# Local attention in blocks of 32 queries and 96 keys, with the probabilities turned on VectorE

## The chip, the core and the metric

The kernel runs on one core of a Trainium2 chip, as one launch. The metric is device time in microseconds, from the start of the program to its end. The core has a matrix engine (TensorE, PE in the profile), VectorE (DVE), ScalarE (ACT), GpSimd (POOL), and a queue on SyncE (SP) that issues transfers. Each engine runs its own instruction stream in order; the streams meet at semaphores.

## The reference, cut to what matters

The input is x, 8 sequences of 1024 rows of 128 numbers. The result comes from three steps, all in fp32:

```
x = x + 1/2 * block(LN(x)); x = x + causal_attention(LN(x)); x = x + 1/2 * block(LN(x))
block: 2 layers of
    h = shift_token(x)                    # the second half of the columns comes from the row before
    q, k, v = split(h @ wqkv)             # 8 heads of 64
    q, k = rotary_xpos(l2norm(q) * qs, l2norm(k) * ks)
    sim = q k^T * 8, masked where key > query or key < query - 64
    x = x + softmax(sim) v @ wo           # wo: 512 x 128
    h = LN(shift_token(x)) * g + b
    a, gate = split(h @ w1 + b1)          # 2 x 341 columns
    x = x + (a * gelu(gate)) @ w2 + b2
```

What the change touches is `softmax(sim) v @ wo`. A query sees itself and the 64 keys before it, 65 keys in all.

## The kernel before

The four local layers (two before the causal attention, two after it) are cut into turns of 256 rows: 32 turns a layer, 128 in all. A loop `local(phase)` on each engine does a *round*, which is two turns, t and t+1; the work of a round is spread over five neighbouring turns (index t-4 to t), so that every engine always has work of several turns at hand. The first and last rounds of each phase, and the causal attention between them, are written out with the same functions. There are 64 pairs of turns in all.

The order of the instructions on each engine is written by hand, as the order of the calls in these loops. The accumulators lie in 8 PSUM banks. The table `ROTA` says which results use a bank in a round, in which order; `vacant` makes PE wait until the engine that reads the former user is done.

The chain of the local attention in one turn, with its lines in the profile:

- `project` (L619 to L621) makes q, k and v of 128 rows, three fp32r matmuls each (high and low parts of both sides). VectorE, POOL and ACT square, rotate and normalise q and k, and `turn` (L628) transposes them on PE into QT2 and KT.
- `scores(t, i)` (L644, L652), for 128 queries and two banks (even heads, odd heads): four bf16 matmuls put the mask into the banks, and 16 fp32 matmuls add q k^T in tiles of 64x64 of the array, each for 64 queries and 128 keys. An fp32 matmul stands in the trace as two records.
- `row_max` (DVE, L2248, one per bank, four a turn), `exp_rows` (ACT, L4440, four of 128x128 per bank), `row_inverse` (DVE, L2254, four a turn) and `scale_p` (POOL, L5792, 128x512) make the probabilities P.
- `turn_p` (PE, L662) transposes P in 16 pieces of 128x128 a turn into four PSUM banks P0 to P3, and `copy_p` (ACT, L4447) copies each bank to PT.
- `copy_v` (ACT, L4430) puts v into VP, and `move_v` (SP, L537 to L543) fills the other 64 partitions of it with three or four transfers of 128 KB a turn, so that 128 keys stand on 128 partitions for each 64 queries.
- `values(t, i)` (L678), twice a turn: 16 fp32 matmuls of 128 keys x 64 columns (32 records) into one bank O0 or O1.
- `split_o` (ACT, L4454) rounds the result to OTH, `rest_of_o` (DVE, L2260) makes the remainder OTL, and `wo` (L690 to L692) does 12 fp32r matmuls a turn.

What follows keeps its work: `turn_rows` and `turn_back` (the transposes around L702 and L718), LN, `to_gate` and `to_up` (L723 to L725), `gelu`, `gate`, `down` (L742), and the transposes of L756.

## Time and profile before

| | |
|---|---|
| median of 3 runs | 2623.92 us (2622.96 to 2627.61) |
| the profiled execution | span 2623.2 us from first to last instruction; no total of its own is given |
| TensorE clock, mean over the span | 0.993 of full speed |
| PE busy | 2558.0 us, 98% |
| VectorE busy | 2376.0 us, 91% |
| ScalarE busy | 2346.8 us, 89% |
| POOL busy | 2056.4 us, 78% |
| DMA, mean busy share of the 16 engines | queue q1 13.1% |
| transfers that lay out V | 480, 128.0 KB each |

The table is from the first part of the page. Busy time is the union of an engine's instructions. A row of the timeline gives the start, the time until the last of the group has ended, and the engine, line and shapes; since instructions of one engine overlap (the next starts before the last has left the pipeline), the cost of one is read from start to start. In a list of waits each row gives the total, the count and the longest.

### The profile page before, as it was taken

The page shows a single profiled execution, that of the slowest core. Times are in us where ns is not written, and L with a number is a line of the kernel's source. Part 1 is how long each engine was busy: PE and PEld are TensorE (multiplying, and loading weights), DVE is VectorE, ACT ScalarE, POOL GpSimd, SP SyncE. Part 2 cuts the span into 40 slices and gives each one's busy share as a digit, 9 for nine tenths or more (in the row PEclk, how much of TensorE's full clock was granted, in tenths as well). Part 3 has the DMA queues.
Part 4 walks back from the last instruction along what each step waited for, and adds up shares of the span by engine and source line. Part 5 has one row for each costly group of instructions (what it writes and reads, how often), then busy time and mean ns, then how long its engine had stood idle before and what let it go on. Part 6 is the DMA issues. An engine that isn't in the chain of part 4 may idle for free.

```text
span 2623.2 us, 80275 instructions
## 1 busy us (share of the span) xinstructions
PE 2558.0 (98%) x29132; PEld 2063.6 (79%) x29132; DVE 2376.0 (91%) x6206; ACT 2346.8 (89%) x7379; POOL 2056.4 (78%) x2185
## 2 busy tenths in 40 slices
PE   5999999999999999998999999999999999999998
PEld 4778777877788888886997777778777788888876
DVE  7999999999999999996888999999998999999995
ACT  5999999999999999995555999999999999999996
POOL 7999999988887877872104999999988888787873
PEclk8999999999999999999999999999999999999999
DMA  4121111111111111110000111111111111111110
GB/s 105 44 51 31 28 38 31 28 28 39 24 32 28 28 42 26 32 28 8 9 1 11 32 28 32 26 38 32 29 24 39 28 32 40 30 40 36 36 40 26
DMA packets 63810, 83.95 MB, mean 32 GB/s; under 512 B 11538, under 2 KB 30652, under 8 KB 63420
## 3 DMA queue, kind: packets, MB, share of 16 engines
q1 hardware_dynamic: 63420, 78.82, 13.1%
q8 instruction: 236, 3.87, 0.6%
q14 instruction: 154, 1.26, 0.2%
HBM read 11.67 MB, written 4.19 MB: 6 GB/s over the span
## 4 chain that ended last, share of the span: by engine, by line
PE 83%; POOL 6%; DVE 5%; ACT 4%; issue 2%; SPq 0%; DMA 0%; ACTq 0%; POOLq 0%; DVEq 0%
PE PS L678 8%; PE PS L662 8%; PE PS L628 7%; PE PS L652 7%; PE PS L619 6%; PE PS L742 6%; PE PS L621 6%; PE PS L620 6%; PE PS L723 4%; PE PS L725 3%; PE PS L724 3%; PE PS L644 3%; PE PS L690 2%; PE PS L853 2%; PE PS L692 2%
## 5 line engine op out<-in xcount | busy, mean ns | idle before, releaser
L4440 ACT ACTIVATE P<-PS,MX 128x128 f32<-128x128 f32 x2048 | 754.3, 430 | 2.1 <-DVE MX L2248 1.2
L5756 POOL TENSOR_TENSOR T<-T,SQ 128x512 f32<-128x512 f32 x512 | 652.1, 1284 | 115.3 <-DVE SQ L2209 111.7
L5792 POOL TENSOR_TENSOR P<-P,RI 128x512 f32<-128x512 f32 x512 | 527.8, 1042 | 73.8 <-DVE RI L2254 71.7
L4440 ACT ACTIVATION_READ_ACCUMULATOR P<-PS,MX 128x1 f32 x2048 | 535.6, 268 | 0.0
L5769 POOL TENSOR_TENSOR T<-T,RN 128x512 f32<-128x512 f32 x512 | 525.9, 1048 | 6.2 <-DVE RN L2242 3.8
L2190 DVE TENSOR_REDUCE SS<-SQ 128x8 f32<-128x512 f32 x512 | 343.8, 681 | 44.6 <-ACT SQ L4395 37.9
L4395 ACT ACTIVATE SQ<-PS 128x512 f32<-128x512 f32 x512 | 338.1, 662 | 45.9 <-PE PS L621 35.0
L619 PE MATMUL PS<-WH,YH 128*128 128x512 f32 x768 | 346.1, 451 | 6.9 <-POOL YL L5745 3.3
L2248 DVE TENSOR_REDUCE MX<-PS 128x4 f32<-128x512 f32 x512 | 345.8, 678 | 6.5 <-PE PS L652 6.3
L2209 DVE TENSOR_TENSOR SQ<-PS,TAB 128x512 f32<-128x512 f32 x512 | 349.1, 682 | 2.3
L2201 DVE TENSOR_TENSOR T<-PS,TAB 128x512 f32<-128x512 f32 x512 | 344.2, 682 | 7.1 <-PE PS L628 3.3
L4447 ACT COPY PT<-PS 128x512 f32<-128x512 f32 x512 | 301.9, 626 | 32.1 <-PE PS L662 32.0
L628 PEld LDWEIGHTS PS<-CST,T 128*128 128x128 f32 x2048 | 238.6, 141 | 88.8 <-issue 54.8
L628 PE MATMUL PS<-CST,T 128*128 128x128 f32 x2048 | 292.4, 275 | 14.0 <-POOL T L5769 13.4
L621 PE MATMUL PS<-WH,YL 128*128 128x512 f32 x768 | 305.3, 397 | 0.0
L620 PE MATMUL PS<-WL,YH 128*128 128x512 f32 x768 | 303.4, 395 | 0.0
L662 PE MATMUL PS<-CST,P 128*128 128x128 f32 x2048 | 296.4, 278 | 3.1 <-POOL P L5792 1.0
L678 PEld LDWEIGHTS PS<-PT,VP 128*64 128x64 f32 x8192 | 249.5, 138 | 28.3 <-issue 28.1
L662 PEld LDWEIGHTS PS<-CST,P 128*128 128x128 f32 x2048 | 229.2, 141 | 52.4 <-issue 22.9
L652 PE MATMUL PS<-KT,QT 64*64 64x128 f32 x8192 | 268.6, 269 | 0.0
L678 PE MATMUL PS<-PT,VP 128*64 128x64 f32 x8192 | 267.3, 224 | 0.0
L652 PEld LDWEIGHTS PS<-KT,QT 64*64 64x64 f32 x8192 | 243.4, 133 | 16.9
(155 smaller groups left out, 5938.4 us busy)
## 6 DMA issues: line engine op xcount, KB each, us to landing
VP<-VP SPq DMA_DIRECT2D x480, 128.0 KB, 2.3
out_dram<-X SPq DMA_DIRECT2D x16, 256.0 KB, 2.6
X<-in_L_attn_x_dram SPq DMA_DIRECT2D x7, 512.0 KB, 4.5
SG<-in_L_ffn_w_dram SPq DMA_DIRECT2D x5, 341.0 KB, 3.0
...
```

The costliest lines, as they stand in the source:

```text
L619: pe.matmul(PS[:, b, :], YH[:, k, :], WH[:, cols], start=True, stop=False)
L620: pe.matmul(PS[:, b, :], YH[:, k, :], WL[:, cols], start=False, stop=False)
L621: pe.matmul(PS[:, b, :], YL[:, k, :], WH[:, cols], start=False, stop=True).then_inc(projected[x], 1)
L628: ins = pe.transpose(PS[:, b, 128 * p:128 * p + 128], T1[:, k, 128 * p:128 * p + 128], ident)
L652: ins = pe.matmul(PS[64 * w:64 * w + 64, bank_of(f"S{2 * i + x}", t), 128 * p:128 * p + 128], QT2[at, s, p, m:m + WIN], KT[at, p, k:k + 12 ...
L662: ins = pe.transpose(PS[:, b, 128 * p:128 * p + 128], P[:, g, p, :], ident)
L678: ins = pe.matmul(PS[64 * x:64 * x + 64, b, 128 * p + m:128 * p + m + WIN], VP[:, s, 2 * i + w, d:d + 64], PT[:, 2 * i + x, p, m:m + WIN], ...
L2209: dve.tensor_tensor(SQ[:, (2 * n + 1 - x) % 3, :].rearrange("p (h t d) -> p h t d", h=HEADS, t=2), PS[:, b, :].rearrange("p (h t d) -> p h ...
L4440: ins = act.activation(P[:, g, p, :], PS[:, b, 128 * p:128 * p + 128], ACT.Exp, bias=MX[:, g, p:p + 1], accum_out=SM[:, g, p:p + 1])
L5756: pool.tensor_tensor(T1[:, k, :], T1[:, k, :], SQ[:, (2 * n + 1 - x) % 3, :], ALU.add).then_inc(added[x], 1)
L5769: pool.tensor_tensor(heads, heads, RN[:, t % 2, i, 8 * x:8 * x + 8].unsqueeze(2).broadcast_to([128, HEADS, DH]), ALU.mult).then_inc(scaled ...
L5792: pool.tensor_tensor(P[:, g], P[:, g], RI[:, g, :].unsqueeze(2).broadcast_to([128, NPAIR, 128]), ALU.mult).then_inc(p_scaled, 1)
```

## The change

Local attention works in blocks of 32 queries and 96 keys where it had 64 queries and 128 keys. In parts:

- `scores`: one mask matmul for each of 8 array tiles (64 rows x 32 columns), 384 columns wide (L583, L585), then 32 fp32 matmuls (64 records) of 96 columns per 128 queries (L591). The tiles of four pairs of heads stand side by side in the array, so that the queries of a head pair lie on 32 partitions of the bank.
- `row_max` and `row_inverse` work on both banks in one instruction, two a turn each (L1502, L1509). `exp_rows` runs over 96 columns, `scale_p` over 384.
- `turn_p` is now on VectorE (L1516): four STREAM_TRANSPOSE a turn, 128x384, which turn each 32x32 piece in place and write PT directly. `copy_p` and the banks P0 to P3 are gone; banks O2 and O3 are new.
- `values(t)` is one call for a turn (L610): 76 or 80 fp32 matmuls (152 or 160 records) of 32 keys, with 32, 64 or 96 columns, in 8 tiles of 32 rows x 64 columns; for each tile the columns of one turn sum to 768 in two passes.
- `copy_v` writes to a staging buffer VT; `move_v(t)` lays it out in a ring VR by 16 transfers of 32 KB a turn (L480). All wait for both copies of the turn; the last eight also wait for `values(t-1)`.
- `wo` is 4 plain fp32 matmuls of 256 columns (8 records, L623). `split_o` copies two banks in one instruction to a double buffer OT. `rest_of_o`, the high and low parts of Wo and `zero_v` are gone.
- The orders of all engines, `ROTA` and its tables are new. The loops run rounds 3 to 31 and 35 to 63 in place of 9 to 31 and 41 to 62.

PE's round is now: K projection of (t-3,1), two turns of (t-4,1), V projection of (t-4,1), `wo(t-5)`, `scores(t-4,1)`, V of (t-3,0), K of (t-2,0), `turn_rows`, V of (t-3,1), two turns, Q of (t-2,0), `scores(t-3,0)`, K of (t-2,1), `turn_back`, `values(t-4)`; then a turn, Q, gate, a turn, gate, V, an LN transpose, `scores(t-3,1)`, gate, up, up, K, up, `wo(t-4)`, `down`, Q, `values(t-3)`, two turns, Q, LN and y transposes, `scores(t-2,0)`.

```diff
+QB, KB = 32, 96
+NB = 128 // QB
+BPC = CH // QB
+BACK = WIN // QB
+RING = 2 * BPC
+PTS, PTW = 2, BPC * KB + 64
...
-ROUNDS = {0: (9, 32), 1: (41, 63)}
+ROUNDS = {0: (3, 32), 1: (35, 64)}
...
-    [("P0", 4), ("P3", 4), ("YT", 4), ("S3", 3), ("V0", 1), ("S3", 2)],
+    [("V0", 3), ("K0", 2), ("O2", 4), ("LT", 1), ("NR", 2), ("O3", 3), ("S1", 2)],
...
-        def move_v(t, i):
-            s = t % 2
-            on.wait_ge(v_copied, TPC * t + i + 1)
-            sp.dma_start(VP[64:128, s, 2 * i, :], VP[0:64, s, 2 * i + 1, :]).then_inc(v_moved[s][i], 16)
-            if i > 0:
-                on.wait_ge(v_copied, TPC * t + 1)
-                sp.dma_start(VP[0:64, s, 2, :], VP[64:128, s, 1, :]).then_inc(v_moved[s][i], 16)
-            elif not first(t):
-                on.wait_ge(v_copied, TPC * t)
-                sp.dma_start(VP[0:64, s, 0, :], VP[64:128, 1 - s, WPC - 1, :]).then_inc(v_moved[s][i], 16)
+        def move_v(t):
+            on.wait_ge(v_copied, TPC * (t + 1))
+            on.wait_ge(valued, t - 1)
...
+            for k in range(NB):
+                if k == NB - BACK:
+                    on.wait_ge(valued, t)
+                for c in range(NPAIR):
+                    sp.dma_start(VR[QB * c:QB * c + QB, slot(t, k):slot(t, k) + NB + 1:NB, :],
+                                 VT[QB * k:QB * k + QB, t % 2, :, 128 * c:128 * c + 128]).then_inc(v_moved[t % 4], 16)
...
-            for w in range(2):
-                v = 1 if first(t) and i == 0 and w == 0 else 0
-                for x in range(2):
-                    at = slice(64 * x, 64 * x + 64)
-                    pe.matmul(PS[64 * w:64 * w + 64, bank_of(f"S{2 * i + x}", t), :], IDB[at, at],
-                              MLOC[at, v].unsqueeze(1).broadcast_to([64, NPAIR, 128]),
-                              start=True, stop=True)
-            for p in range(NPAIR):
-                for w in range(2):
...
+            for x in range(2):
+                at, rows = slice(64 * x, 64 * x + 64), slice(64 * x, 64 * x + QB)
+                for c in range(NPAIR):
+                    to = PS[QB * c:QB * c + QB, bank_of(f"S{2 * i + x}", t), 0:NB * KB]
...
+                        pe.matmul(to, IDB[at, rows], MLOC[at, 0].rearrange("p n k -> p (n k)"), start=True, stop=True)
+            for n in range(NB):
+                for c in range(NPAIR):
                     for x in range(2):
                         at = slice(64 * x, 64 * x + 64)
-                        k, m = t % 2 * CH + 128 * i + WIN * w, 128 * i + WIN * w
-                        ins = pe.matmul(PS[64 * w:64 * w + 64, bank_of(f"S{2 * i + x}", t), 128 * p:128 * p + 128],
-                                        QT2[at, s, p, m:m + WIN], KT[at, p, k:k + 128], start=False, stop=True,
+                        k, m = t % 2 * CH + 128 * i + QB * n, 128 * i + QB * n
+                        ins = pe.matmul(PS[QB * c:QB * c + QB, bank_of(f"S{2 * i + x}", t), KB * n:KB * n + KB],
+                                        QT2[at, s, c, m:m + QB], KT[at, c, k:k + KB], start=False, stop=True,
                                         skip_group_check=True)
...
-        def turn_p(t, g):
-            b = bank_of(f"P{g}", t)
-            on.wait_ge(p_scaled, GPC * t + g + 1)
-            vacant(on, f"P{g}", t)
-            for p in range(NPAIR):
-                ins = pe.transpose(PS[:, b, 128 * p:128 * p + 128], P[:, g, p, :], ident)
-            ins.then_inc(p_turned, 1)
-
-        def values(t, i):
-
-            s, b = t % 2, bank_of(f"O{i}", t)
-            on.wait_ge(v_copied, TPC * t + i + 1)
-            on.wait_ge(v_moved[s][i], v_moves(t, i))
-            if i == 0 and first(t):
-                on.wait_ge(v_zero, t // CPB + 1)
-            on.wait_ge(p_copied, GPC * t + 2 * i + 2)
-            vacant(on, f"O{i}", t)
-            for p in range(NPAIR):
-                for w in range(2):
+        def values(t):
+
+            on.wait_ge(v_moved[t % 4], moved(t))
+            on.wait_ge(p_turned, GPC * (t + 1))
+            for half in range(2):
+                vacant(on, f"O{2 * half}", t)
+                vacant(on, f"O{2 * half + 1}", t)
+            begin = 0 if first(t) else -BACK
+            for b in range(begin, BPC):
+                lo, hi = max(b, 0), min(b + BACK, BPC - 1)
+                at = 2 * QB * lo + QB * (b + BACK)
+                for c in range(NPAIR):
                     for x in range(2):
-                        d, m = 64 * (2 * p + x), WIN * w
-                        ins = pe.matmul(PS[64 * x:64 * x + 64, b, 128 * p + m:128 * p + m + WIN],
-                                        VP[:, s, 2 * i + w, d:d + 64], PT[:, 2 * i + x, p, m:m + WIN], start=True,
-                                        stop=True)
+                        keys = PT[QB * c:QB * c + QB, t % PTS, x, at:at + 64 * (hi + 1 - lo)]
+                        ins = pe.matmul(PS[64 * x:64 * x + 64, o_banks(t, c // 2)[c % 2], QB * lo:QB * hi + QB],
+                                        VR[QB * c:QB * c + QB, slot(t, b), 64 * x:64 * x + 64],
+                                        keys.rearrange("p (n k) -> p n k", k=64)[:, :, 0:QB],
+                                        start=b == begin, stop=True, skip_group_check=True)
             ins.then_inc(valued, 1)
 
         def wo(t):
...
-            on.wait_ge(wo_lo, 1)
-            on.wait_ge(o_copied, TPC * (t + 1))
+            on.wait_ge(wo_in, DEPTH * 16)
+            on.wait_ge(o_copied, 2 * (t + 1))
...
             for p in range(NPAIR):
-                pe.matmul(PS[:, b, half:half + CH], WOH[:, wl, p, :], OTH[:, p, :], start=(p == 0), stop=False)
-                pe.matmul(PS[:, b, half:half + CH], WOL[:, wl, p, :], OTH[:, p, :], start=False, stop=False)
-                ins = pe.matmul(PS[:, b, half:half + CH], WOH[:, wl, p, :], OTL[:, p, :], start=False,
+                ins = pe.matmul(PS[:, b, half:half + CH], WO[:, wl, p, :], OT[:, t % 2, p, :], start=(p == 0),
                                 stop=(p == NPAIR - 1))
...
-        def row_max(t, g):
-            on.wait_ge(exped, GPC * (t - 1) + g + 1)
-            on.wait_ge(scored, TPC * t + g // 2 + 1)
-            dve.tensor_reduce(MX[:, g, :], PS[:, bank_of(f"S{g}", t), :].rearrange("p (n k) -> p n k", n=NPAIR), AX.X,
+        def row_max(t, i):
+            b0, b1 = s_banks(t, i)
+            on.wait_ge(exped, GPC * (t - 1) + 2 * i + 2)
+            on.wait_ge(scored, TPC * t + i + 1)
+            dve.tensor_reduce(MX[:, 2 * i:2 * i + 2, :],
+                              PS[:, b0:b1 + 1:b1 - b0, 0:NB * KB].rearrange("p b (n k) -> p b n k", n=NB), AX.X,
                               ALU.max, negate=True).then_inc(maxed, 1)
 
-        def row_inverse(t, g):
-            on.wait_ge(p_scaled, GPC * (t - 1) + g + 1)
-            on.wait_ge(exped, GPC * t + g + 1)
-            dve.reciprocal(RI[:, g, :], SM[:, g, :]).then_inc(inverted, 1)
-
-        def rest_of_o(t, i):
-            on.wait_ge(o_hi, TPC * t + i + 1)
-            dve.tensor_tensor(OTL[:, :, 128 * i:128 * i + 128],
-                              PS[:, bank_of(f"O{i}", t), :].rearrange("p (n k) -> p n k", n=NPAIR),
-                              OTH[:, :, 128 * i:128 * i + 128].bitcast(F32), ALU.subtract).then_inc(o_copied, 1)
+        def row_inverse(t, i):
+            on.wait_ge(p_scaled, GPC * (t - 1) + 2 * i + 2)
+            on.wait_ge(exped, GPC * t + 2 * i + 2)
+            dve.reciprocal(RI[:, 2 * i:2 * i + 2, :], SM[:, 2 * i:2 * i + 2, :]).then_inc(inverted, 1)
+
+        def turn_p(t, g):
+            i, x = g // 2, g % 2
+            on.wait_ge(valued, t + 1 - PTS)
+            on.wait_ge(p_scaled, GPC * t + g + 1)
+            to = PT[:, t % PTS, x, KB * NB * i:KB * NB * (i + 1)].rearrange("p (n k) -> p n k", n=NB)
+            dve.transpose(to, P[:, g, :, 0:KB]).then_inc(p_turned, 1)
...
         def copy_v(t, i):
-            s = t % 2
...
+            if t >= 2:
+                on.wait_ge(v_moved[(t - 2) % 4], moved(t - 2))
             on.wait_ge(projected[V], TPC * t + i + 1)
-            act.copy(VP[:, s, 2 * i + 1, :], PS[:, bank_of(f"V{i}", t), :]).then_inc(v_copied, 1)
+            act.copy(VT[:, t % 2, i, :], PS[:, bank_of(f"V{i}", t), :]).then_inc(v_copied, 1)
...
-                ins = act.activation(P[:, g, p, :], PS[:, b, 128 * p:128 * p + 128], ACT.Exp, bias=MX[:, g, p:p + 1],
+                ins = act.activation(P[:, g, p, 0:KB], PS[:, b, KB * p:KB * p + KB], ACT.Exp, bias=MX[:, m, p:p + 1],
...
-        def copy_p(t, g):
-            on.wait_ge(valued, TPC * (t - 1) + g // 2 + 1)
-            on.wait_ge(p_turned, GPC * t + g + 1)
-            act.copy(PT[:, g].rearrange("p n k -> p (n k)"), PS[:, bank_of(f"P{g}", t), :]).then_inc(p_copied, 1)
-
-        def split_o(t, i):
...
-            on.wait_ge(wo_mm, t)
-            on.wait_ge(valued, TPC * t + i + 1)
-            act.copy(OTH[:, :, 128 * i:128 * i + 128],
-                     PS[:, bank_of(f"O{i}", t), :].rearrange("p (n k) -> p n k", n=NPAIR)).then_inc(o_hi, 1)
+        def split_o(t, half):
+            b0, b1 = o_banks(t, half)
...
+            on.wait_ge(wo_mm, t - 1)
+            on.wait_ge(valued, t + 1)
+            act.copy(OT[:, t % 2, 2 * half:2 * half + 2, :], PS[:, b0:b1 + 1:b1 - b0, 0:CH]).then_inc(o_copied, 1)
...
         def scale_p(t, g):
-            if g == 0:
-                zero_v(t)
-            on.wait_ge(inverted, GPC * t + g + 1)
-            pool.tensor_tensor(P[:, g], P[:, g], RI[:, g, :].unsqueeze(2).broadcast_to([128, NPAIR, 128]),
+            on.wait_ge(inverted, TPC * t + g // 2 + 1)
+            rows = P[:, g, :, 0:KB]
+            pool.tensor_tensor(rows, rows, RI[:, g, :].unsqueeze(2).broadcast_to([128, NB, KB]),
                                ALU.mult).then_inc(p_scaled, 1)```

On PE, the place where the values of one turn are multiplied, before (PS<-CST,P are the transposes of P, PS<-PT,VP the values, PS<-NH,W1H the gate):

```order
L619 MATMUL PS<-WH,YH 128x512
L620 MATMUL PS<-WL,YH 128x512
L621 MATMUL PS<-WH,YL 128x512
L628 MATMUL PS<-CST,T 128x128 x4
L662 MATMUL PS<-CST,P 128x128 x8
L678 MATMUL PS<-PT,VP 64x64 x32
L723 MATMUL PS<-NH,W1H 128x512
```

And after (PS<-PT,VB are the values, PS<-CST,T the transposes of q and k):

```order
L556 MATMUL PS<-WH,YH 128x512
L557 MATMUL PS<-WL,YH 128x512
L558 MATMUL PS<-WH,YL 128x512
L610 MATMUL PS<-PT,VB 64x32 x8
L610 MATMUL PS<-PT,VB 64x64 x8
L610 MATMUL PS<-PT,VB 64x96 x48
L610 MATMUL PS<-PT,VB 64x64 x8
L610 MATMUL PS<-PT,VB 64x32 x8
L565 MATMUL PS<-CST,T 128x128 x8
```

The transposes of P have left PE, and a turn's values are 80 matmuls in a row where they were 32.

On VectorE, between the steps of the root (RN, RR), before: two reciprocals and the two remainders of the attention's result.

```order
L2254 RECIPROCAL RI<-SM 128x4 [waits exped,p_scaled]
L2232 SCALAR_TENSOR_TENSOR PS<-RN,PS 128x32 [waits normed]
L2254 RECIPROCAL RI<-SM 128x4 [waits exped,p_scaled]
L2234 TENSOR_TENSOR PS<-PS,RN 128x32 [waits normed]
L2260 TENSOR_TENSOR OTL<-PS,OTH 128x4x128 [waits o_hi]
```

After, at the end of the same root, the second half of the round, with the four transposes of one turn:

```order
L1516 STREAM_TRANSPOSE PT<-P 128x384 [waits p_scaled,valued]
L1573 SCALAR_TENSOR_TENSOR G<-PS,COLS,G 85x512 [waits gelued,up_mm]
L1491 TENSOR_SCALAR RR<-PS 128x32 [waits normed]
L1516 STREAM_TRANSPOSE PT<-P 128x384 [waits p_scaled]
L1509 RECIPROCAL RI<-SM 128x8 [waits exped]
L1493 TENSOR_TENSOR PS<-PS,RR 128x32 [waits normed]
L1443 TENSOR_REDUCE SS<-SQ 128x8 [waits sq_k]
L1516 STREAM_TRANSPOSE PT<-P 128x384 [waits p_scaled]
L1495 SCALAR_TENSOR_TENSOR RN<-PS,RN 128x32 [waits normed]
L1516 STREAM_TRANSPOSE PT<-P 128x384 [waits p_scaled]
```

VectorE no longer waits for ACT's rounding of the result (o_hi); it waits for POOL (p_scaled), which waits for VectorE's reciprocal three rows earlier.

On the transfer queue, two turns of moves before:

```order
L537 DMA VP<-VP 64x512 [waits v_copied]
L540 DMA VP<-VP 64x512
L537 DMA VP<-VP 64x512 [waits v_copied] x2
L540 DMA VP<-VP 64x512
```

And after:

```order
L480 DMA VB<-VB 32x2x128 [waits v_copied]
L480 DMA VB<-VB 32x2x128 x7
L480 DMA VB<-VB 32x2x128 [waits valued]
L480 DMA VB<-VB 32x2x128 x7
```

The second is one turn alone: eight transfers once V is copied, eight more once the turn before has been multiplied.

## Rows read from the trace of the kernel before

**Rows 1.** Part 4 of the page, the chain that ended last, by engine:
```profile
PE 83%; POOL 6%; DVE 5%; ACT 4%; issue 2%; SPq 0%; DMA 0%; ACTq 0%; POOLq 0%; DVEq 0%
```

**Rows 2.** Windows, five rounds: length, each engine's busy time (count), granted clock, DMA share:
```profile
242.98:427.13 184.15, 183.77 (x2161) 146.62 (x2160) 175.35 (x474) 176.26 (x564) 168.21 (x184) 1.00 0.14 32
```

**Rows 3.** Timeline of PE in one round, 316.60 to 353.50:
```profile
324.01 0.41 PE L644 MATMUL PS<-MLOC,IDB 64*64 64x512 bf16 x4
324.25 1.04 PE L652 MATMUL PS<-KT,QT 64*64 64x128 f32 x32
325.23 0.66 PE L662 MATMUL PS<-CST,P 128*128 128x128 f32 x4
325.64 0.36 PE L690 MATMUL PS<-OTH,WOH 128*128 128x256 f32 x1
...
327.16 0.40 PE L619 MATMUL PS<-WH,YH 128*128 128x512 f32 x1
...
329.51 2.08 PE L678 MATMUL PS<-PT,VP 128*64 128x64 f32 x64
331.52 0.50 PE L723 MATMUL PS<-NH,W1H 128*128 128x512 f32 x1
...
340.94 2.74 PE L742 MATMUL PS<-G,W 128*128 128x512 f32 x6
343.52 1.04 PE L628 MATMUL PS<-CST,T 128*128 128x128 f32 x8
344.39 0.38 PE L756 MATMUL PS<-CST,XN 128*128 128x128 f32 x2
```

**Rows 4.** Line L644: durations of one instruction, least, median, most, in ns:
```profile
L644 PE MATMUL PS<-MLOC,IDB x1024: 372/400/401, 37.5 to 2582.8; 64*64 64x512 bf16 x171
```

**Rows 5.** Timeline of VectorE in the same round:
```profile
332.66 0.17 DVE L2254 RECIPROCAL RI<-SM 128x4 f32<-128x4 f32 x1
332.75 0.66 DVE L2260 TENSOR_TENSOR OTL<-PS,OTH 128x512 fp32r<-128x512 f32 x1
333.32 0.17 DVE L2254 RECIPROCAL RI<-SM 128x4 f32<-128x4 f32 x1
...
349.86 0.88 DVE L2292 BATCH_NORM_STATS2 RST<-PS 128x6 f32<-128x128 f32 x4
350.65 0.67 DVE L2248 TENSOR_REDUCE MX<-PS 128x4 f32<-128x512 f32 x1
351.25 0.37 DVE L2298 BATCH_NORM_AGGREGATE RMV<-RST 128x2 f32<-128x6 f32 x4
```

**Rows 6.** Waits in the five rounds of rows 2: total us, times, longest:
```profile
DVE SS L2190 <- ACT SQ L4395: 2.1, 5, 0.4
...
DVE RI L2254 <- ACT P L4440: 1.7, 5, 0.3
```

**Rows 7.** Timeline of ACT in the same round:
```profile
329.13 1.13 ACT L4447 COPY PT<-PS 128x512 f32<-128x512 f32 x2
330.10 0.67 ACT L4395 ACTIVATE SQ<-PS 128x512 f32<-128x512 f32 x1
...
347.82 0.40 ACT L4406 COPY KT<-PS 128x256 f32<-128x256 f32 x1
348.09 0.63 ACT L4407 COPY KT<-PS 128x512 f32<-128x512 f32 x1
```

**Rows 8.** Timeline of POOL in the same round:
```profile
318.12 0.47 POOL L5745 TENSOR_TENSOR YL<-Y,YH 128x128 fp32r<-128x128 f32 x1
318.54 3.06 POOL L5769 TENSOR_TENSOR T<-T,RN 128x512 f32<-128x512 f32 x3
```

**Rows 9.** Timeline of the transfer queue:
```profile
283.32 0.46 SPq L537 DMA_DIRECT2D VP<-VP  x1
283.83 0.60 SPq L540 DMA_DIRECT2D VP<-VP  x1
```

**Rows 10.** Part 6 of the page: transfers, count, KB each, median us to landing:
```profile
VP<-VP SPq DMA_DIRECT2D x480, 128.0 KB, 2.3
```

More of the change, by code:

```diff
@@ L470, in within, with moved, slot, s_banks @@
         return 2 * u % CPB * CH
-    def v_moves(t, i):
-        if i == 0 and t % 2 == 0:
-            return 16 * (t // CPB * 3 + (1 if first(t) else 3))
-        return 32 * (t // 2 + 1)
+    def moved(t):
+        return 16 * NPAIR * NB * (t // 4 + 1)
+    def slot(t, b):
+        return (t % 2 * BPC + b) % RING
+    def s_banks(t, i):
+        return sorted(bank_of(f"S{2 * i + x}", t) for x in range(2))
+    def o_banks(t, half):
+        return sorted(bank_of(f"O{2 * half + k}", t) for k in range(2))
     def part_stage(l, n):
@@ L590, in _ @@
             if t >= 0:
-                for i in range(TPC):
-                    move_v(t, i)
+                move_v(t)
                 if t == TURN - 1:
@@ L897, in first_steps @@
+            wo(0)
+            scores(1, 1)
             project(3, 0, K)
+            project(3, 0, Q)
+            values(1)
+            turn(2, 0, K)
             turn(2, 0, Q)
[L899 to L902 removed]
+            project(3, 1, Q)
+            turn_ln(4)
             scores(2, 0)
[L904 to L908 removed]
@@ L1232, in local @@
-                turn_y(s - 4)
-                values(t - 4, 0)
-                values(t - 4, 1)
-                project(t - 2, 0, V)
+                project(t - 2, 0, Q)
+                scores(t - 3, 0)
+                project(t - 2, 1, K)
+                turn_back(s - 3)
+                values(t - 4)
+                turn(t - 3, 1, K)
+                project(t - 2, 1, Q)
+                to_gate(s - 3, 0)
+                turn(t - 3, 1, Q)
+                to_gate(s - 3, 1)
+                project(t - 2, 0, V)
@@ L2029, in last_steps @@
+            wo(2 * TURN - 4)
+            down(2 * PAIRS - 3)
             project(2 * TURN - 1, 0, Q)
+            turn(2 * TURN - 2, 0, K)
+            values(2 * TURN - 3)
+            turn_y(2 * PAIRS - 3)
             turn(2 * TURN - 2, 0, Q)
-            project(2 * TURN - 2, 1, V)
-            project(2 * TURN - 1, 1, Q)
-            project(2 * TURN - 1, 1, K)
-            turn(2 * TURN - 2, 0, K)
-            turn_back(2 * PAIRS - 3)
-            turn(2 * TURN - 2, 1, K)
-            scores(2 * TURN - 2, 0)
@@ L4565, in a_copy_far @@
             act.copy(PTF[i % 4][:, 512:512 + n], PS[:, A_TURN[1], 0:n]).then_inc(a_pcB, 1)
+        for n in range(4):
+            stage_wa(0, n)
         def first_steps():
```

5246 lines of the change are left out of this document (1206 added, 4040 removed), and 188 rows, old and new, of tables (FIRST_USERS, LAST_USERS, ROTA).

## The prediction

> **What bounds the kernel now.** I read the chain that ended last first: PE holds 83% of it [rows 1]. The windows then tell how close the others are. Over five rounds of 36.83 us (184.15 / 5), PE is busy for 183.77 of 184.15 us at a granted clock of 1.00, and VectorE 175.35, ACT 176.26, POOL 168.21 [rows 2]. So a round is PE's time, but with 35.07 us of VectorE, 35.25 of ACT and 33.64 of POOL right below it: relief of PE alone is worth at most 1.6 us a round, and what VectorE is given or spared counts as much. The timelines give the cost of one instruction, read from start to start, and the waits say whom VectorE waits for.
>
> **PE, per round (two turns).** Removed: 32 transposes of P. Eight of the same kind take 344.39 - 343.52 = 0.87 us, 0.109 each [rows 3]: -3.5.
>
> Scores: a block takes 325.23 - 324.01 = 1.22 us, 0.24 for four masks of 512 columns and 0.98 for 32 records, which are 8 steps of four array tiles with 128 columns [rows 3]. After, the mask is 384 columns (0.18) and 64 records are 8 steps of eight tiles with 96 columns: 0.98 x 96/128 = 0.74. This needs eight tiles to run at once. The nearest row: four masks, 0.400 us each alone [rows 4], end within 0.41 together [rows 3], so they start at most 0.01 us apart and a group of eight is under way before its 0.09 us are over. I take 0.95 a block: 4 x -0.27 = -1.1.
>
> Values: 64 records take 331.52 - 329.51 = 2.01 us a turn, 32 steps of two tiles with 64 columns, 0.98 ns a column [rows 3]. After, 768 columns a tile in two passes: 1536 x 0.98 = 1.5 us. Two turns: -0.9 or so.
>
> Wo: 12 records took 327.16 - 325.64 = 1.52 us. A plain fp32 record costs (343.52 - 340.94) / 6 = 0.43 us for 512 columns [rows 3], so eight of 256 take 1.72: +0.4 for two turns.
>
> PE's work: 36.83 - 3.5 - 1.1 - 0.9 + 0.4 = 31.7 us. At four tiles at a time it is 37.7 (below); that is the upper end.
>
> **VectorE, per round.** 512 elements cost 351.25 - 350.65 = 0.60 us, 128 cost (350.65 - 349.86) / 4 = 0.198 [rows 5]: 1.05 ns an element and 0.06 fixed. Maxima: eight of 512 (4.8) become four of 768 (0.87 each, 3.5): -1.3. Reciprocals: eight of 0.09 [rows 5] become four of 0.1: -0.3. Remainders: four of 333.32 - 332.75 = 0.57 [rows 5]: -2.3. Added: eight transposes of 384 elements. The trace has none. At one element per step, as all the rows of this engine, 0.47 each; the low end is 0.27 (half the slope), the high end 0.87 (twice). I take 0.47, since every shape there is lies on that slope: +3.7. Sum: 35.07 - 1.3 - 0.3 - 2.3 + 3.7 = 34.9 us busy.
>
> To it belongs idle time. Now it is 36.83 - 35.07 = 1.76 a round, of which (2.1 + 1.7) / 5 = 0.76 are waits for ACT's squares and exponentials [rows 6]; the other 1.0 is small gaps between dependent steps of the root. ACT gets emptier (below), so I let the 0.76 go and keep the 1.0: 35.9. New is the chain exponential, reciprocal (VectorE), scaling (POOL), transpose (VectorE), through which VectorE waits for POOL with its own later work queued behind: sums of squares, the last gate, `y_next`. The order puts a gate, a root step or a sum between the two, and POOL needs about 0.8 us per scaling.
>
> **ACT, POOL, the transfer queue.** ACT loses eight copies of P at (330.10 - 329.13) / 2 = 0.485 us, 3.9, and, at (0.485 - 0.27) / 256 = 0.84 ns an element, 32 exponentials of 32 elements less, 0.9 [rows 7]: 35.25 - 4.8 = 30.5. POOL: (1.02 - 0.42) / 384 = 1.56 ns an element [rows 8], eight scalings shorter by 128: 33.6 - 1.6 = 32.0. Neither sets the round.
>
> The queue issues 32 transfers a round in place of seven or eight. One issue takes 283.83 - 283.32 = 0.51 us, and 0.60 at most [rows 9]; 16 are 8.2 to 9.6 us a turn, 16 to 19 a round: it keeps up, but each turn's V is late. In the round, V of (t-4,1) is projected 2.5 us after PE begins, and its copy stands behind two squares, copies and exponentials; I put it at 4.6. Then 8.2 us of issues and 2.3 to landing [rows 10]: 15.1. PE reaches `values(t-4)` after seven of its twelve projections, two of four score blocks, four of eight turns and one `wo`, about 12.0 us: it waits 3.1, and with 19.7 left ends at 34.8. VectorE's fourth transpose for that turn stands at about 15, too. So PE's wait is real but smaller than its gain, and VectorE ends last, at 35.9.
>
> **Sum.** 64 pairs of turns x (36.83 - 35.9 = 0.93) = 60 us. The ends of each phase and the causal attention keep their work; I give them nothing, plus or minus 10. The profile gives the execution's span, 2623.2, and the median of the runs is 2623.92, 0.7 above, so the span can stand for the run: 2623.9 - 60 = 2564 us.
>
> **The rivals.**
>
> *VectorE's transpose is slow.* At twice the slope, eight cost 3.2 us more: round 39.1, 64 x 2.3 = +145, 2769 us. For it: it reads and writes in another pattern than any row. Against: all rows, of reductions too, lie on one slope. 9%. The Trainium skill ("VectorE: DVE Perf Modes", "The three transpose paths") gives 311 ns for a 128x128 bf16 transpose on VectorE in blocks of 32x32; with the slope of rows 5 for 256 elements more it would be an estimate of 0.58 us each, and then a round of 36.8. No row here shows a transpose on that engine.
>
> *PE waits for V and for the hand-overs (the slower side).* Place: `values(t-4)` and `values(t-3)`. At 0.60 an issue V lands at 4.6 + 9.6 + 2.3 = 16.5, 4.5 us after PE gets there; and the second half's fourth transpose, behind ACT's last exponential, the reciprocal and two scalings, holds `values(t-3)` for another 1.3: 31.7 + 5.8 = 37.5 a round, +43, 2667 us. It decides from 36.83 - 31.7 = 5.1 us of waits on PE a round. For it: the second of a pair of issues is the 0.60 one [rows 9], and the last eight transfers of a turn wait for the values before. Against: small transfers may be issued faster, and a wait in one round is partly made up in the next. 15%.
>
> *The small tiles do not run eight at a time.* Rows show four (scores) and two (values). At four, scores cost 0.74 more a block and values 1.5 more a turn: 31.7 + 3.0 + 3.0 = 37.7, +56, 2680. At the 0.031 us a record of today (2.01 / 64 and 0.98 / 32 [rows 3]), a block takes 2.2 and a turn's values 5.0: about 43.5 a round, +427, 3051. Against both: 0.031 is just what the columns need at two and four tiles, and the masks start within 0.01. 11% in all. The Trainium skill ("TensorE: Matmul & The Clock Gate", "Back-to-back issue gap") speaks for the slow side: about 25 ns an instruction as a floor up to 64 columns, which by an estimate from it makes 160 records 4.0 us a turn; the masks' starts do not agree with it across tiles. The same page ("Part 3: Packing small matmuls") puts 4 ns between tiles that run together, by which the sum would be mine.
>
> *No change.* VectorE keeps its 0.76 of waits and gets 0.2 more: 34.9 + 1.0 + 0.96 = 36.9. 5%.
>
> **How the numbers follow.** My case 60%; the rivals 9, 15, 11 and 5. Its own range is 2507 to 2616, from a VectorE round of 35.0 (cheap transposes or gaps gone, 64 x 1.83 = 117) to one of 36.7. Lower still, a round of 34.8 gives 2494. Upwards the range takes in the late V and the four tiles, to 2700; left out are the slow transpose, the slow records and a rest, under 2 in 10. Within 0.2% (5 us), about what can be told from no change here, is 5%; faster is my case, 60%; slower the three others, 35%.
>
> **What would show it.** Windows in steady rounds of 35.9 us with VectorE busy 34.9 and PE 31.7 to 32; transposes of 384 elements 0.47 from start to start; a values group of 1.5 us and a score block of 0.95; PE idle about 3 us before `values(t-4)`, put down to the transfers or to VectorE; ACT near 30.5. I am wrong if PE's values take over 3 us a turn, if a transpose takes over 0.6, or if PE waits over 5 us a round.

## The result, and the profile after

| | before | after |
|---|---|---|
| median | 2623.98 us | 3039.3 us (3035.5 to 3043.75, 4 runs) |
| ratio | | 1.158 (95% interval 1.157 to 1.160) |
| span of the profiled execution | 2623.2 | 3039.7 (its run 3041.49) |

The change makes the kernel 415 us slower. 2564 was forecast, with a range to 2700.

The page after, parts 1 and 4 (compare [rows 1]):

```profile
PE 2547.1 (84%) x47052; PEld 1935.4 (64%) x47052; DVE 2371.1 (78%) x5957; ACT 2075.1 (68%) x6870; POOL 1928.3 (63%) x2152
...
PE 51%; SPq 20%; ACT 14%; issue 6%; DMA 4%; DVE 2%; POOL 1%; ACTq 0%; POOLq 0%; DVEq 0%
SPq L480 20%; PE PS L610 11%; ACT P L2647 6%; PE PS L673 5%; PE PS L565 5%; DMA VB<-VB 4%; PE PS L556 4%; PE PS L623 4%; PE PS L654 3%; PE PS L557 3%; PE PS L558 3%; PE PS L591 3%; PE PS L655 2%; PE PS L656 2%; PE PS L784 2%
```

A queue that was in no chain now holds a fifth of it. The group of the values in part 5 of the page has 278.8 us of PE's idle time in front of it, 233.3 of them put down to the transfers of V:

```profile
L610 PE MATMUL PS<-PT,VB 32*64 32x96 f32 (+1 forms) x19456 | 327.1, 292 | 278.8 <-DMA VB<-VB 233.3
```

Over 25 rounds, windows of before and then of after (columns as in [rows 2]):

```profile
263.58:1178.28 914.70, 913.41 (x10789) 733.06 (x10788) 852.22 (x2167) 874.40 (x2784) 774.03 (x818) 1.00 0.14 31
```

```profile
283.73:1354.64 1070.91, 911.85 (x17777) 683.82 (x17776) 849.55 (x2082) 767.66 (x2587) 730.11 (x814) 0.92 0.13 29
```

A round went from 36.59 to 42.84 us; 64 of them are 400 of the 415 us. PE is busy for as long as before (36.54, now 36.47) where 31.7 was forecast, and idle for 6.36 us a round (0.05 before). VectorE (33.98), ACT (30.7) and POOL (29.2) are all well below the round: no engine is full. The chain shows what is, from ACT's copy of V to the values (start, us, what):

```profile
301.61 0.49 ACT VB L2636
302.10 0.02 issue
302.12 0.58 SPq L480
302.71 0.04 issue
302.75 0.60 SPq L480
...
309.14 1.65 SPq L480
...
312.75 1.91 DMA VB<-VB
314.65 0.04 issue
314.70 2.73 PE PS L610 x126
```

Sixteen issues, 0.64 us from one to the next but for one of 1.65, start from 302.12 to 312.75; the last lands 1.9 after its start. The sixteen of the next turn follow at once, so that the queue is busy for 22 us of the round. PE's timeline over the same stretch answers to [rows 3]:

```profile
307.55 0.36 PE L585 MATMUL PS<-MLOC,IDB 64*32 64x384 bf16 x8
307.73 0.97 PE L591 MATMUL PS<-KT,QT 64*32 64x96 f32 x64
309.14 0.50 PE L556 MATMUL PS<-WH,YH 128*128 128x512 f32 x1 [0.44 <-POOL YL L3261]
...
310.02 0.63 PE L649 MATMUL PS<-CST,G 128*128 128x128 f32 x4
314.70 2.73 PE L610 MATMUL PS<-PT,VB 32*64 32x96 f32 x128 [4.04 <-DMA VB<-VB]
317.36 1.11 PE L565 MATMUL PS<-CST,T 128*128 128x128 f32 x4
318.12 0.78 PE L556 MATMUL PS<-WH,YH 128*128 128x512 f32 x1
318.70 0.63 PE L557 MATMUL PS<-WL,YH 128*128 128x512 f32 x1
319.12 0.63 PE L558 MATMUL PS<-WH,YL 128*128 128x512 f32 x1
...
322.32 0.39 PE L557 MATMUL PS<-WL,YH 128*128 128x512 f32 x1
...
333.74 2.07 PE L610 MATMUL PS<-PT,VB 32*64 32x32 f32 x160
```

PE stands for 4.04 us; over the 25 rounds it waits for V's transfers 3.65 us a round. What follows is slow: a projection's matmul lasts 0.63 us at 319 and 0.39 at 322. The values at 314.7 belong to the first turn of a sequence, which has 64 matmuls (128 records, not the 152 of the section on the change) where the others have 80 (160): 2.73 us here, 1.74 in e1 below without the wait; a turn of 160 records takes 3.17 behind such a wait and 2.07 at 333.7. The windows of after give the reason in the column before the last two:

```profile
306.00:310.00 4.00, 3.52 (x86) 2.46 (x85) 3.93 (x14) 3.90 (x13) 3.92 (x7) 1.00 0.27 58
310.00:314.00 4.00, 0.66 (x5) 0.42 (x4) 3.92 (x10) 3.73 (x18) 4.00 (x4) 1.00 0.16 34
314.00:318.00 4.00, 3.30 (x131) 3.24 (x132) 1.98 (x6) 0.48 (x1) 2.42 (x4) 0.53 0.26 58
318.00:322.00 4.00, 4.00 (x16) 3.22 (x15) 0.69 (x1) 1.84 (x5) 1.27 (x1) 0.62 0.21 45
```

After the wait the granted clock is 0.53 and then 0.62 of full, that is, most of the time the lower level, 1.2 GHz; before the wait it was 1.00. So one wait is paid twice.

VectorE did what was forecast. Its timeline (compare [rows 5]):

```profile
309.81 0.56 DVE L1516 STREAM_TRANSPOSE PT<-P 128x384 f32<-128x384 f32 x1
310.29 0.65 DVE L1462 TENSOR_TENSOR SQ<-PS,TAB 128x512 f32<-128x512 f32 x1
```

A transpose costs 0.48 to 0.50 from start to start; 0.47 was forecast.

### The profile page after: what moved, and what is told of

The parts are those of the page before. It is cut to its first block, busy times and chain, and to the rows that moved or that the text cites. A ratio compares the mean times of both kernels' runs of the same rounds, so it can differ in the third digit from the quotient of the medians.

```text
span 3039.7 us, 116197 instructions
## 1 busy us (share of the span) xinstructions
PE 2547.1 (84%) x47052; PEld 1935.4 (64%) x47052; DVE 2371.1 (78%) x5957; ACT 2075.1 (68%) x6870; POOL 1928.3 (63%) x2152
## 3 DMA queue, kind: packets, MB, share of 16 engines
q8 instruction: 373, 6.11, 0.8%
## 4 chain that ended last, share of the span: by engine, by line
PE 51%; SPq 20%; ACT 14%; issue 6%; DMA 4%; DVE 2%; POOL 1%; ACTq 0%; POOLq 0%; DVEq 0%
SPq L480 20%; PE PS L610 11%; ACT P L2647 6%; PE PS L673 5%; PE PS L565 5%; DMA VB<-VB 4%; PE PS L556 4%; PE PS L623 4%; PE PS L654 3%; PE PS L557 3%; PE PS L558 3%; PE PS L591 3%; PE PS L655 2%; PE PS L656 2%; PE PS L784 2%
## 5 line engine op out<-in xcount | busy, mean ns | idle before, releaser
L2647 ACT ACTIVATE P<-PS,MX 128x96 f32<-128x96 f32 x2048 | 674.4, 359 | 11.8 <-DVE MX L1502 8.1
L610 PE MATMUL PS<-PT,VB 32*64 32x96 f32 (+1 forms) x19456 | 327.1, 292 | 278.8 <-DMA VB<-VB 233.3
L3286 POOL TENSOR_TENSOR P<-P,RI 128x384 f32<-128x384 f32 x512 | 417.6, 827 | 198.4 <-DVE RI L1509 198.3
L610 PEld LDWEIGHTS PS<-PT,VB 32*64 32x64 f32 x19456 | 309.2, 166 | 322.2 <-DMA VB<-VB 252.7
L556 PE MATMUL PS<-WH,YH 128*128 128x512 f32 x768 | 401.2, 522 | 112.4 <-ACT VB L2636 50.7
L1443 DVE TENSOR_REDUCE SS<-SQ 128x8 f32<-128x512 f32 x512 | 343.1, 675 | 186.5 <-ACT SQ L2606 186.4
L2647 ACT ACTIVATION_READ_ACCUMULATOR P<-PS,MX 128x1 f32 x2048 | 460.5, 225 | 0.0
L2657 ACT COPY OT<-PS 128x512 f32<-128x512 f32 x256 | 137.5, 589 | 393.2 <-PE PS L610 393.2
L1462 DVE TENSOR_TENSOR SQ<-PS,TAB 128x512 f32<-128x512 f32 x512 | 347.6, 679 | 4.6
L565 PE MATMUL PS<-CST,T 128*128 128x128 f32 x2048 | 328.3, 298 | 22.8 <-ACT OT L2657 13.1
L557 PE MATMUL PS<-WL,YH 128*128 128x512 f32 x768 | 314.2, 409 | 0.0
L558 PE MATMUL PS<-WH,YL 128*128 128x512 f32 x768 | 314.1, 409 | 0.0
L565 PEld LDWEIGHTS PS<-CST,T 128*128 128x128 f32 x2048 | 255.3, 152 | 73.6 <-issue 34.4
L1516 DVE STREAM_TRANSPOSE PT<-P 128x384 f32<-128x384 f32 x512 | 290.4, 568 | 13.5 <-POOL P L3286 5.2
L556 PEld LDWEIGHTS PS<-WH,YH 128*128 128x128 f32 x768 | 154.3, 201 | 217.1 <-issue 102.5
L1502 DVE TENSOR_REDUCE MX<-PS 128x8 f32<-128x768 f32 x256 | 243.3, 950 | 27.1 <-PE PS L591 23.6
L3261 POOL TENSOR_TENSOR YL<-Y,YH 128x128 fp32r<-128x128 f32 x256 | 111.2, 435 | 241.4 <-ACT YH L2600 239.2
L591 PE MATMUL PS<-KT,QT 64*32 64x96 f32 x16384 | 250.0, 246 | 0.0
```

The costliest lines, as they stand in the source:

```text
L556: pe.matmul(PS[:, b, :], YH[:, k, :], WH[:, cols], start=True, stop=False)
L557: pe.matmul(PS[:, b, :], YH[:, k, :], WL[:, cols], start=False, stop=False)
L558: pe.matmul(PS[:, b, :], YL[:, k, :], WH[:, cols], start=False, stop=True).then_inc(projected[x], 1)
L565: ins = pe.transpose(PS[:, b, 128 * p:128 * p + 128], T1[:, k, 128 * p:128 * p + 128], ident)
L610: ins = pe.matmul(PS[64 * x:64 * x + 64, o_banks(t, c // 2)[c % 2], QB * lo:QB * hi + QB], VR[QB * c:QB * c + QB, slot(t, b), 64 * x:64 * ...
L1462: dve.tensor_tensor(SQ[:, (2 * n + 1 - x) % 3, :].rearrange("p (h t d) -> p h t d", h=HEADS, t=2), PS[:, b, :].rearrange("p (h t d) -> p h ...
```

## The experiments

Rounds, busy and idle time of PE are from a window of 25 steady rounds of each kernel, as above. Where the text says for what PE waited, in us a round, it is the idle time in front of PE's instructions in these windows, by the engine or transfer that ended it.

| kernel | median us | ratio to before (95%) | round | PE busy | PE idle |
|---|---|---|---|---|---|
| before | 2624 | | 36.59 | 36.54 | 0.05 |
| after | 3039.3 | 1.157 to 1.160 | 42.84 | 36.47 | 6.36 |
| e1 two transfers | 2764.5 | 1.051 to 1.058 | 38.30 | 34.72 | 3.58 |
| e2 filled wait | 3005.7 | 1.143 to 1.147 | 42.33 | 38.60 | 3.73 |
| e3 V by PE | 2826.7 | 1.076 to 1.080 | 39.48 | 35.94 | 3.54 |
| e4 V first | 2853.2 | 1.083 to 1.090 | 39.44 | 35.08 | 4.37 |
| e5 before, Wo alone | 2650.2 | 1.008 to 1.011 | 37.01 | 36.97 | 0.04 |
| e7 values later | 2956.5 | 1.125 to 1.128 | 41.50 | 35.80 | 5.70 |
| e8 = e4 and e7 | 2992.1 | 1.138 to 1.141 | 42.05 | 35.93 | 6.12 |
| e9 = e3 and e7 | 2975.1 | 1.131 to 1.136 | 41.92 | 36.76 | 5.17 |
| e10 = e1, half the values | 2642.8 | 1.005 to 1.008 | 36.32 | 32.71 | 3.60 |
| e11 = e1, short maximum | 2742.8 | 1.043 to 1.047 | 38.00 | 34.15 | 3.85 |
| e12 = e3, short maximum | 2794.3 | 1.062 to 1.069 | 39.01 | 35.50 | 3.51 |
| e13 before, short maximum | 2623.6 | 0.999 to 1.000 | 36.59 | 36.54 | 0.05 |
| e14 = e3, swaps | 2988.7 | 1.136 to 1.142 | 42.20 | 36.41 | 5.78 |
| e15 = e12, swaps | 2909.2 | 1.107 to 1.112 | 40.85 | 35.75 | 5.10 |
| e16 = e1, swaps | 2938.3 | 1.117 to 1.125 | 41.08 | 35.22 | 5.85 |

**The way of V.** First the issues are taken away, then the wait is filled, then the transfers go altogether, then V is made earlier.

e1:

```diff
-            for k in range(NB):
-                if k == NB - BACK:
-                    on.wait_ge(valued, t)
-                for c in range(NPAIR):
-                    sp.dma_start(VR[QB * c:QB * c + QB, slot(t, k):slot(t, k) + NB + 1:NB, :],
-                                 VT[QB * k:QB * k + QB, t % 2, :, 128 * c:128 * c + 128]).then_inc(v_moved[t % 4], 16)
+            sp.dma_start(VR[:, first_slot:first_slot + 6, :], flat[:, 0:6, :]).then_inc(v_moved[t % 4], 16)
+            on.wait_ge(valued, t)
+            sp.dma_start(VR[:, first_slot + 6:first_slot + 8, :], flat[:, 6:8, :]).then_inc(v_moved[t % 4], 16)
```

> The changed kernel, with V moved to the ring by 2 transfers a turn (384 KB, then 128 KB after the values of the turn before) in place of 16 of 32 KB: same bytes, same waits, but the rows land on the partitions they come from, so the values are multiplied with wrongly placed keys; the arithmetic has the same shapes. Theory A (the 16 issues at 0.64 us each and their landing lie in the loop that sets the round, and PE's wait for them brings the clock down): the wait of 4.0 us before values(t-4) goes, the granted clock stays at 1.00, and a round falls from 42.8 to 36 us: about 2610 us. Theory B (the small tiles and the hand-overs between the engines set the round, and V is only the last of several late inputs): another wait takes its place, round 40 or more: over 2860 us.

Measured 2764.5, 275 us less than after, between the two theories. The wait for V is gone, and with it the slow clock behind it (mean 0.99). So the issues, with what follows from them, are 275 of the 415 us; the other 140 are not theirs. Against before, e1 has 1.8 us a round less work on PE and 3.5 more of idle time. Its transfer queue, with only two issues a turn:

```profile
707.22 0.47 SPq L478 DMA_DIRECT2D VB<-VB  x1
707.73 0.60 SPq L480 DMA_DIRECT2D VB<-VB  x1
713.09 0.47 SPq L478 DMA_DIRECT2D VB<-VB  x1
```

A first issue lasts 0.47, one right behind another 0.60, as in [rows 9], where the prediction took the first's step for all. In after even the first of a burst, on a queue that had been idle for 20 us, lasts 0.58: its small transfers are never issued at 0.47 (least 0.585 of 800).

e2:

```diff
-            on.wait_ge(v_moved[t % 4], moved(t))
-            on.wait_ge(p_turned, GPC * (t + 1))
             for half in range(2):
...
+            if t % 2 == 0:
+                for _ in range(16):
+                    pe.matmul(PS[:, o_banks(t, 0)[0], 0:128], ident, ident, start=True, stop=True)
+            on.wait_ge(v_moved[t % 4], moved(t))
+            on.wait_ge(p_turned, GPC * (t + 1))
```

> The changed kernel, with 16 matmuls of the identity with itself (fp32, 128x128, about 3.5 us) put before the wait for V of every even turn, into a bank that the values then overwrite. PE still waits for V but not idle. Theory A says the wait stays and that the time lost to it at 1.2 GHz (the values at 2.7 us where 2.0 are seen at full clock, and the six matmuls of 512 columns after it at 0.42 in place of 0.23) comes back: 2 to 3 us a round, about 2870 us. If the slow clock costs nothing because VectorE or ACT are behind anyway, the time stays at 3039 within 20 us. If V lands earlier than I think, the fill itself costs and it gets slower.

Measured 3005.7: faster by 34, a miss in size (about 170 was expected). PE's timeline has the values at full clock (2.06, where after has 3.17 for the same 160 records):

```profile
788.13 3.81 PE L603 MATMUL PS<-CST 128*128 128x128 f32 x32 [0.68 <-ACT P L2650]
792.30 2.06 PE L613 MATMUL PS<-PT,VB 32*64 32x32 f32 x160 [0.36 <-DMA VB<-VB]
```

PE busy is 38.60, of it 3.8 filling: 34.8 of real work where after has 36.47. So the slow clock costs 1.7 us a round, 107 us in all. But the filling replaces only 6.36 - 3.73 = 2.6 us of idle time with 3.8 of its own, 1.2 more than it fills: 1.7 - 1.2 = 0.5 us a round are left, the 34.

e3 (in `project`, for V; ACT copies the bank straight to a ring of 32 slots, and `values` waits for that copy):

```diff
+            if x == V:
+                for n in range(NB):
+                    rows = slice(columns(t, i) + QB * n, columns(t, i) + QB * n + QB)
+                    for c in range(NPAIR):
+                        at = 128 * c
+                        ins = pe.matmul(PS[QB * c:QB * c + QB, b, 128 * n:128 * n + 128], Y0[:, rows],
+                                        WV[:, at:at + 128], start=True, stop=True,
+                                        skip_group_check=True)
+                ins.then_inc(projected[x], 1)
+                return
```

> The changed kernel without any transfer for V: PE projects V in plain fp32 straight onto the partitions where the values need it (per 128 rows 16 matmuls of 32 rows x 128 columns in four column strips of the array, in place of three of 128x512), and ACT copies the bank to a ring of 32 slots. Theory A: V is there when the bank is copied, no wait, clock 1.00; PE gets 0.3 us a turn more (1024 columns a strip in two passes at 0.84 ns, 1.7 us, for 1.4 now). A round of 35 to 37, 2560 to 2660 us, about 2600. Theory B: 40 or more a round, over 2860 us, since it has even more small tiles.

Measured 2826.7: 213 us better than after, with V in its right places, but well over the 2600 of theory A. It lies above e1 by PE's work (35.94 against 34.72): summed from start to start, V's small matmuls take 2.07 us a turn, not 1.7.

e4 (the V projection of (t-4,1) first in the loop on PE, its copy on ACT ahead of a square, two copies and eight exponentials):

> The changed kernel, with two calls moved in the loop: PE projects V of (t-4,1) as the first thing of the round (three calls earlier, about 1.6 us), and ACT copies it before a square, two copies and eight exponentials (about 3 us earlier). Theory A: V lands about 2.7 us earlier in the round, PE's wait shrinks by as much and the slow stretch behind it too: round 39 to 40, 2800 to 2870 us. Theory B: no more than 0.5 us a round, over 3000 us.

Measured 2853.2, 186 us for moving two calls; the wait for V's transfers falls from 3.65 us a round to 0.13. So theory A holds for the way of V, and e1, e3 and e4 show its limit: 3.5 us or more of PE's idle time stay.

**What is left without the wait for V.** e10 leaves out the values of every other block of keys, e11 takes work from VectorE; both are e1 otherwise.

```diff
-                for c in range(NPAIR):
+                for c in range(NPAIR) if b % 2 == 0 else ():
```

> The kernel with two transfers a turn (2764 us, 38.4 us a round), with the values of every other block of keys left out: 40 matmuls a turn in place of 80, so the result is not the reference's. Each turn's values should take about 1.0 us in place of 2.0. If PE's own work and its fetching of instructions set the rest of the excess, a round gets 2 to 2.5 us shorter: 36 to 36.4, about 2610 to 2640 us, and the pauses of PE in the middle of the values (1.7 us each, in some rounds) get fewer. If VectorE's chain of hand-overs sets it, under 1 us a round: over 2700.

```diff
-                              PS[..., 0:NB * KB].rearrange("p b (n k) -> p b n k", n=NB), AX.X,
+                              PS[..., 0:NB * KB].rearrange("p b (n k) -> p b n k", n=NB)[:, :, :, 48:80], AX.X,
```

> The kernel with two transfers a turn (2764 us), with the row maximum taken over 32 of the 96 keys, which every query of a block sees or has masked with at least one seen among them (softmax does not change with the shift). VectorE's four maxima a round fall from 0.87 to about 0.33 us: 2.2 us less of 34.9, and each stands in the chain from the scores to the exponentials. If VectorE's chain sets the rest of the excess: 1.5 to 2.5 us a round, 2600 to 2670 us. If PE's work sets it: under 0.5 us a round, over 2730.

e10 measured 2642.8: 1.98 us a round, all of it PE's busy time, while the idle time stayed (3.60). e11 measured 2742.8: 0.3 us a round for 2.2 less of VectorE. So the round follows PE's own work and hardly VectorE's, with some 3.6 us of idle time beside it. In e1 these are 0.84 us a round for ACT's copy of V out of a bank, 0.82 for VectorE's last transpose (0.10 in after, where the wait for V covered it), 0.68 of pauses, 0.46 for POOL's YL and smaller ones. The pauses stand inside a run of matmuls that waits for nothing. PE's timeline of e1:

```profile
732.20 1.92 PE L609 MATMUL PS<-PT,VB 32*64 32x32 f32 x147
735.78 0.34 PE L609 MATMUL PS<-PT,VB 32*64 32x32 f32 x13 [1.66 <-issue]
```

There are 28 of them over 0.5 us in e1 (42 us, the longest 1.98), 27 in after (34 us), 33 in e3 (49 us), none before and none in e10. The instruction queue in part 3 of the page, of after and of e10:

```profile
q8 instruction: 373, 6.11, 0.8%
```

```profile
q8 instruction: 297, 4.87, 0.8%
```

Packets and MB; before had 236 and 3.87, e3 has 431 and 7.06. That the pauses are waits for this queue can be told from the times in the traces: in after and in e1 a packet of q8 starts 2.2 to 3.0 us before the end of every one of the pauses (27 of 27, 28 of 28), whatever their length, and a moment taken anywhere in the span has one there in one case in ten. What they cost is less plain: e10 has none of them and yet the same idle time as e1, since other waits are longer there (0.40 for VectorE's NL, 0.34 for ACT's KT).

> V laid out by PE (2827 us) and the row maximum over 32 of the 96 keys. The same question on a kernel without any transfer for V: VectorE sets it: 2680 to 2740; PE sets it: over 2790. Against the kernel before it should still be slower.

Measured 2794.3, 32 us better than e3, or 0.5 us a round for 2.0 less of VectorE: PE sets that kernel, too.

**Waits that come back.** e7 puts `values(t-4)` four calls later on PE; e8 and e9 do the same to e4 and e3.

```diff
                 turn_back(s - 3)
-                values(t - 4)
                 turn(t - 3, 1, K)
                 project(t - 2, 1, Q)
                 to_gate(s - 3, 0)
                 turn(t - 3, 1, Q)
+                values(t - 4)
                 to_gate(s - 3, 1)
```

> The changed kernel, with values(t-4) four calls later on PE (behind a transpose of k, the Q projection, a gate and a transpose of q: about 2.4 us of work that does not need V), and on ACT the two copies of the result behind the copies of k and q and a square. Theory A: PE's wait of 4.0 us shrinks to about 1.5, and the slow stretch with it: 39 to 40 us a round, 2800 to 2870 us. Theory B (V's lateness is a symptom: what comes before V's copy in the loop is late by as much): 42 us or more, 3000 us.

> Both orders together: V projected and copied first in the round (e4: 2853 us) and values(t-4) four calls later. Theory A: no wait for V is left, and the round falls to what it is with two transfers (38.4 us, 2764 us) or a little below, since the wait for VectorE's last transpose (0.7 us) is covered, too: 2730 to 2770 us. If the two orders only move the same wait about, 2830 or more.

> V laid out by PE (2827 us), with values(t-4) four calls later. In that kernel PE waits about 1.2 us a round for VectorE's last transpose before the values, and the clock falls now and then behind it. Covered, a round of 39.3 falls to 37.5 to 38: 2720 to 2760 us. If PE's own work bounds it (the small matmuls of V and of the values), no more than 0.5 us a round: over 2790.

e7 gained 83 us, less than half of what theory A expected, and e8 and e9 lost 139 and 148 against e4 and e3. In e7 the wait for V did fall, from 3.65 us a round to 0.14, but a new one of 2.10 stands in its place, the same as in e9 (2.11) and e8 (2.11). PE's timeline of e9:

```profile
736.51 1.01 PE L562 MATMUL PS<-CST,T 128*128 128x128 f32 x4 [2.13 <-DVE NL L1562]
```

The transpose of k uses the bank of `turn_back` (HB, then TK1 in `ROTA`), which VectorE has to read first; the values had stood between the two. The wait that they covered is now open.

e16, e14 and e15 swap two neighbours twice (`project(t - 3, 1, V)` ahead of `project(t - 2, 0, K)`, `turn_back` ahead of `project(t - 2, 1, K)`):

> The kernel with two transfers a turn (2764 us, PE idle for 3.6 us of a 38.3 us round), with two neighbours swapped twice on PE: the V projection of (t-3,1) goes ahead of K of (t-2,0), which waits 0.8 us a round for its bank (the V of (t-3,0) has to be copied out first), and turn_back ahead of K of (t-2,1), which waits 0.4 us for POOL. If PE's waits are each a matter of where one call stands: 1.2 us a round less, about 2690 us. If a wait that is covered comes back at the next hand-over (as when the values went four calls later: 2853 to 2992 us): within 20 us of 2764.

> The same two swaps on the kernel in which PE lays V out (2827 us). By the first reading about 2760 us, by the second 2810 to 2840.

> The same, with the row maximum over 32 keys (that alone was worth 32 us here): 2725 us by the first reading, 2780 to 2810 by the second. In both it stays slower than the kernel before.

All three got slower, by 174, 162 and 115 us, which neither reading had. PE's timeline of e16:

```profile
719.13 0.50 PE L555 MATMUL PS<-WH,YH 128*128 128x512 f32 x1 [2.46 <-DVE T L1453]
```

By `ROTA`, V of (t-3,1) uses the bank of Q1, the Q of the same rows, which was projected late in the round before and which VectorE reads late: a wait of 0.8 us for one bank became one of 2.5 for another. The other swap cost as well: `turn_back`, one call earlier, waits 1.29 us a round for ACT's G (0.31 in after). The order and the table of banks hold each other; no swap tried here frees PE.

**One part alone.**

> The kernel before, with one part of the change alone: Wo in plain fp32 (4 matmuls of 256 columns a turn in place of 12 in high and low parts), the attention's result copied in fp32 to a double buffer, no remainder on VectorE. By my sum PE gets 0.4 us a round more and VectorE 2.3 less. If PE alone sets the round, as the profile of before says: +0.4 x 64 = +26, 2650 us. Rival: PE's 57 us of idle time in the whole span are waits for this part of the chain (7.1 + 4.7 us of them in 1000 us are put down to the remainders), and go with it: 2620 to 2630.

Measured 2650.2, as forecast: 0.42 us a round. Summed from start to start, only 0.15 of it stand in Wo's own matmuls (3.04, now 3.19); the rest stands in the first matmul of 512 columns behind them, twice a round, which took 0.23 us behind the old Wo and takes 0.42 behind the plain fp32 one. VectorE's relief (852 to 797 us in 25 rounds) is worth nothing there.

> The kernel before, with the row maximum over 32 of the 128 keys of each block: eight maxima a round fall from 0.60 to about 0.20 us, 3.2 us less of VectorE's 35.1. By the profile of before PE alone sets the round and VectorE's relief is worth only what PE waits for it (57 us of idle time in the span, most of it pauses under 0.4 us that no engine is named for): 2605 to 2625 us.

Measured 2623.6 (ratio 0.999 to 1.000): VectorE falls from 852.22 to 781.61 us in 25 rounds, and the round stays 36.59. So it is PE that bounds before, and VectorE does not.

## Why the prediction was wrong

The step that failed is the comparison in "PE's wait is real but smaller than its gain, and VectorE ends last, at 35.9". The gain of 5.1 us a round was not there: PE is busy for 36.47 us, not 31.7, so that every wait lengthened the round, and PE ends last, not VectorE. The wait for V, which the forecast put at 3.1, is 3.65 a round; to it come 2.7 of other idle time, for which the forecast named no cause. Of its own signs of being wrong, "if PE waits over 5 us a round" came true. Point by point, in us a round:

- *The V path.* Forecast from the start of PE's round: copy at 4.6, issues 8.2, landing 2.3, in all 15.1. Measured: PE's round starts at 296.3, the copy ends at 302.1 (5.8), issues 10.6, landing 1.9: 18.3. PE reached the values after 14.4, not 12.0, so the wait was 4.04 in the round shown. The second rival had V later than the forecast, at 16.5, and has the right mechanism; its price, 2667, was far too low, since it too took PE's work at 31.7.
- *PE's gain.* Forecast 31.7, measured 36.47. Summed from start to start over 25 rounds: the transposes of P are gone (3.5, right); the values take 4.9 for both turns (forecast 3.1, before 4.0), 3.9 of it at full clock (e1), the rest the slow clock; scores 4.4 (3.8); Wo 3.6 (3.44). In a turn of values of e1, eight records of 32 columns take 0.05 to 0.08 us where the forecast's 0.98 ns a column gives 0.03, and eight of 96 columns 0.08 to 0.13 where it gives 0.09. The matmuls that the change does not touch take 2.5 more than before, 1.7 of it still in e1. Of the 1.7, 1.4 stand in the first and third matmul of a projection or a gate and 0.06 in the second, that is, where one kind of work follows another: before, the first takes 0.23 behind another projection or gate and 0.32 to 0.34 behind transposes, scores or values. Why the seams cost more in the new order stays open. The prediction had no term for that, nor for the clock, which goes down when PE waits. e2 puts the clock at 1.7.
- *The small tiles* were no failure of principle: 160 records in 2.07 us are 0.013 each, against 0.031 before, so they do run side by side. Both slow forms of that rival are out, and the time of 3051 that one of them gave is near the result by accident. In e1's values, records of 32 columns in neighbouring tiles start 6 to 8 ns apart. The floor of some 25 ns a matmul of the Trainium skill ("TensorE: Matmul & The Clock Gate", "Back-to-back issue gap") does not hold for matmuls in different tiles here.
- *VectorE.* Transposes 0.48 (0.47), busy time 0.1 less than before (0.2 forecast). The low slope was right, and the rival of a slow transpose is out. But VectorE is not the bound; e11 shows that 2.2 us of it are worth 0.3.
- *Hand-overs.* PE idle for 3.6 us even in e1 was not forecast at all. Before has 0.05: its order had PE's inputs ready. The new one does not, and e7 to e9 and e14 to e16 show that the waits move when a call moves.

In sum, 42.84 - 35.9 = 6.9 us a round: 4.8 more of PE's work (of which 1.7 the clock), and idle 6.36 where 4.2 was implied. By experiment: 275 us are the sixteen issues with what follows from them (e1), and half of the values' matmuls are worth 122 us (e10). The pauses without a wait are 34 us of after's idle time; what a kernel without them would gain was not tested. What each of e1's waits would give back, taken away alone, stays open, as does an order made anew for this kernel.
